# The selective-scan stage: TensorE's and ScalarE's loop over chunks written out in full, and the C rows loaded in quarters that GpSimd waits for one by one

## What is computed

```python
A = -jnp.exp(A_log)                     # (512 channels, 64 states)
C_used = C_ssm[:, jnp.arange(L) % 128, :]

def step(h, inp):
    dt, b, xt, c = inp
    dA = jnp.exp(dt[:, :, None] * A)
    h = dA * h + dt[:, :, None] * b[:, None, :] * xt[:, :, None]
    y = jnp.einsum('bdn,bn->bd', h, c)
    return (h, y)
...
return (y + x * D_param) @ out_proj_w.T
```

## Time and profile before

| | |
|---|---|
| time, median of 3 runs | 8651.39 us (8645.66 to 8653.18) |
| time of the profiled execution | 8648.8 us, its span 8647.0 us |
| TensorE busy | 7638.4 us (88%) |
| VectorE busy | 6621.9 us (77%) |
| GpSimd busy | 5670.5 us (66%) |
| ScalarE busy | 4702.7 us (54%) |
| scan stage, from its first scan to its last `reduce` | about 594.8 to 5550 us |

### The profile page before, as it was taken

How to read it: one execution, slowest core, us unless ns; L and a number is a source line. 1 busy time by engine, 2 the same in 40 slices (tenths; PEclk the granted TensorE clock), 3 DMA queues, 4 the chain that set the end, 5 groups by cost and what they waited for, 6 DMA issues and landing times. The chain is left out here.

```text
span 8647.0 us, 222908 instructions
## 1 busy us (share of the span) xinstructions
PE 7638.4 (88%) x76550; PEld 5615.1 (65%) x76550; DVE 6621.9 (77%) x8318; ACT 4702.7 (54%) x10584; POOL 5670.5 (66%) x3272
## 2 busy tenths in 40 slices
PE   5659999999989989989999999899999989999984
PEld 3337777777777777777777777644444436666653
DVE  4439999999999999999999999622222237878776
ACT  4447777777777777777777787511111112222220
POOL 0009999999999999999999999600000015554544
PEclk8779999999999999999999999999999988988885
DMA  3350000000000000000000000121221222222215
GB/s 134 137 158 0 20 21 0 20 21 1 19 21 20 0 21 20 0 21 20 8 13 20 20 0 5 60 83 68 87 82 68 92 79 78 76 79 74 79 66 168
DMA packets 198786, 423.53 MB, mean 49 GB/s; under 512 B 22448, under 2 KB 48496, under 8 KB 183024
## 3 DMA queue, kind: packets, MB, share of 16 engines
q1 hardware_dynamic: 172768, 382.77, 13.2%
q10 hardware_dynamic: 25872, 38.80, 1.2%
HBM read 225.11 MB, written 196.41 MB: 49 GB/s over the span
## 5 line engine op out<-in xcount | busy, mean ns | idle before, releaser
L485 POOL TENSOR_TENSOR scan_hc<-scan_h,scan_cb 128x1024 f32<-128x1024 f32 x2048 | 4776.9, 2366 | 265.8 <-DMA scan_cb<-scratch_bc 127.5
L651 DVE TENSOR_TENSOR_SCAN scan_h<-scan_a,scan_carry,scan_u 128x512 f32<-128x512 f32 x4096 | 4802.1, 1260 | 156.0 <-PE scan_u L590 128.1
L590 PE MATMUL scan_u<-scan_dg,scan_v 64*128 64x128 f32 x32768 | 2391.7, 286 | 339.1 <-DVE scan_h L651 280.1
L536 ACT ACTIVATE scan_a<-scan_dt,scan_aneg 128x512 f32<-128x512 f32 x4096 | 2659.9, 708 | 44.8 <-issue 30.5
L590 PEld LDWEIGHTS scan_u<-scan_dg,scan_v 64*128 64x128 f32 x32768 | 2000.7, 188 | 819.1 <-DVE scan_h L651 538.0
L598 PE MATMUL scan_y<-scan_ident,scan_hc 128*128 128x128 f32 x16408 | 2251.0, 280 | 60.1 <-POOL scan_hc L485 33.6
L598 PEld LDWEIGHTS scan_y<-scan_ident,scan_hc 128*128 128x128 f32 x16408 | 1764.8, 141 | 310.3 <-POOL scan_hc L485 34.5
L507 ACT ACTIVATE scan_dg<-scan_half,scan_bt 128x64 f32<-128x64 f32 x4096 | 1139.2, 341 | 5.0 <-DVE scan_onward L634 5.0
L528 ACT ACTIVATE scan_carry<-scan_h,scan_onward 128x4 f32 (+1 forms) x1008 | 303.0, 301 | 1042.5 <-DVE scan_h L651 1042.5
L177 POOL TENSOR_TENSOR mid_r<-mid_ve,mid_half_neg 128x4 f32<-128x4 f32 x32 | 32.4, 1012 | 1271.4 <-DVE mid_ve L132 784.1
L1141 POOL TENSOR_TENSOR core_joint<-core_own 128x32 f32<-128x32 f32 x64 | 17.4, 272 | 621.2 <-DVE core_own L1271 536.6
(11 more groups left out here) (211 smaller groups left out, 7647.3 us busy)
## 6 DMA issues: line engine op xcount, KB each, us to landing
scratch_y<-scan_yo ACTq DMA_DIRECT2D x17, 1024.0 KB, 4.7
pre_x<-in_x SPq DMA_DIRECT2D x16, 1024.0 KB, 6.8
scratch_z<-pre_zt SPq DMA_DIRECT2D x16, 1024.0 KB, 3.9
scratch_dt<-pre_dt SPq DMA_DIRECT2D x16, 1024.0 KB, 4.6
scratch_vr<-pre_vr ACTq DMA_DIRECT2D x16, 1024.0 KB, 4.7
scan_dt<-scratch_dt SPq DMA_DIRECT2D x16, 1024.0 KB, 5.3
scan_v<-scratch_vr SPq DMA_DIRECT2D x32, 512.0 KB, 7.8
scan_z<-scratch_z SPq DMA_DIRECT2D x16, 1024.0 KB, 10.7
```

The source lines that it names most:

```text
L485: pool.tensor_tensor(hc[:, q].rearrange("p n (r j) -> p n r j", j=P), h[:, q].rearrange("p n (r j) -> p n r j", j=P), cb[:, bass.ds(b * NS ...
L536: ins = act.activation(a[:, q, n, :], dt[:, par, q, :], ACT.Exp, scale=aneg[:, q, bass.ds(m * 2 + n, 1)])
L590: mm = pe.matmul(u_ps[:, q % 2, g, k * HP:(k + 1) * HP, :], v[row, par, k, q, :], dg[row, buf, k], start=True, stop=True)
L651: ins = dve.tensor_tensor_scan(h[:, q, n, :], a[:, q, n, :], u_ps[:, q % 2, :, :, n].rearrange("p g t -> p (g t)"), carry[:, q, bass.ds(m ...
```

## The change

`by_chunk` no longer has a loop: all 16 chunks of TensorE's and ScalarE's program are written out, with a constant number in each. The inner loops over pairs stay. The load of C is cut: each 4 MB transfer becomes four of 1 MB (16 states each), with a semaphore for each of the first sequence's quarters and one for all of the second sequence's; the second sequence's are issued behind the inputs of chunk 1. GpSimd's first chunk becomes four loops of 8 pairs, each behind the wait for its quarter, and its wait for the second sequence's C stands in front of chunk 8.

```diff
@@ scan_phase
+    PARTS = 4
+    PART = NS // PARTS
-        y_out = sem("y_out"); cb_in = sem("cb_in"); z_used = sem("z_used")
+        y_out = sem("y_out"); cb_in = [sem(f"cb_in{i}") for i in range(PARTS)]; cb_rest = sem("cb_rest"); z_used = sem("z_used")
-        def by_chunk(eng, chunk):
-
-            if NCH > 2:
-                with eng.Fori(0, NCH // 2 - 1) as p:
-                    for par in range(2):
-                        chunk(p * 2 + par, par, p, False)
-            for par in range(2):
-                chunk(NCH - 2 + par, par, NCH // 2 - 1, par == 1)
+        def by_chunk(chunk):
+
+            for c in range(NCH):
+                chunk(c, c % 2, c // 2, c == NCH - 1)
             load(0, 0)
-            for b in range(B):
-                sp.dma_start(cb[:, b * NS:(b + 1) * NS, :], bc_s[b * KC, HP:HP + NS, 0:P].partition_broadcast(P)).then_inc(cb_in, 16)
+
+            def load_c(b, n):
+                sp.dma_start(cb[:, b * NS + n * PART:b * NS + (n + 1) * PART, :], bc_s[b * KC, HP + n * PART:HP + (n + 1) * PART, 0:P].partition_broadcast(P)).then_inc(cb_rest if b else cb_in[n], 16)
+            for n in range(PARTS):
+                load_c(0, n)
             load(1, 1)
+            for b in range(1, B):
+                for n in range(PARTS):
+                    load_c(b, n)
...
             pool.sem_inc(hc_ready, Q)
-            pool.wait_ge(cb_in, 16 * B)
             pool.wait_ge(filled, 5)
-            with pool.Fori(0, B) as b:
-                with pool.Fori(0, KC) as k:
-                    with pool.Fori(0, PAIRS) as m:
-                        for q in range(Q):
-                            i = (b * KC + k) * PER + m * Q + q
+
+            def items(c, b, first, pairs):
+                with pool.Fori(0, pairs) as k:
+                    m = first + k
+                    for q in range(Q):
+                        i = c * PER + m * Q + q
...
+            for n in range(PARTS):
+                pool.wait_ge(cb_in[n], 16)
+                items(0, 0, n * (PAIRS // PARTS), PAIRS // PARTS)
+            for b in range(B):
+                if b:
+                    pool.wait_ge(cb_rest, 16 * PARTS * (B - 1))
+                with pool.Fori(b == 0, KC) as k:
+                    items(b * KC + k, b, 0, PAIRS)
```

More of the change, by code:

```diff
@@ L472, in _ @@
             pool.sem_inc(hc_ready, Q)
-            pool.wait_ge(cb_in, 16 * B)
             pool.wait_ge(filled, 5)
-            with pool.Fori(0, B) as b:
-                with pool.Fori(0, KC) as k:
-                    with pool.Fori(0, PAIRS) as m:
-                        for q in range(Q):
-                            i = (b * KC + k) * PER + m * Q + q
[L481 to L489, removed]
+            def items(c, b, first, pairs):
[3 more added lines that the diff above has]
+                        i = c * PER + m * Q + q
+                        pool.wait_ge(h_ready, i + Q + 1)
+                        pool.wait_ge(hc_used, i + 1)
+                        hold(pool, ticks["pool"])
+                        pool.tensor_tensor(
+                            hc[:, q].rearrange("p n (r j) -> p n r j", j=P),
+                            h[:, q].rearrange("p n (r j) -> p n r j", j=P),
+                            cb[:, bass.ds(b * NS + m * 2, 2), :].rearrange("p n (x j) -> p n x j", x=1).broadcast_to([P, 2, T // P, P]), ALU.mult
+                        ).then_inc(hc_ready, 1)
+            for n in range(PARTS):
[6 more added lines that the diff above has]
+                    items(b * KC + k, b, 0, PAIRS)
         @block.scalar
@@ L562, in _ @@
             diagonals(0, 0, 0, [(k, n) for k in range(K) for n in range(2)]).then_inc(dg_ready, 1)
-            by_chunk(act, chunk)
+            by_chunk(chunk)
             copy_out(NCH)
@@ L621, in chunk @@
                         reduce((c + 1) * PER - Q + q, q)
-            by_chunk(pe, chunk)
+            by_chunk(chunk)
         @block.vector
```

## The result

The changed kernel takes 8542.07 us (median of 4 runs, 8539.83 to 8550.57), the kernel before 8650.39 us: ratio 0.9877, with a 95% interval of 0.986 to 0.9894, 108 us less. Run anew it took 8544.76 against 8651.33 us, ratio 0.9876 (0.9861 to 0.9891). The forecast was 8549, 101.8 us less.

A forecast was written before the change was run, and what follows sets the result against it. VectorE's path was taken to bound the scan stage. Outer loop 69.2 plus C in quarters 32.6 gave 101.8 us off the profiled 8648.8, 8547.0, plus 2.6 to the median: 8549 us, own range 8540 to 8560, wider range 8538 to 8583.

The forecast's parts named there:

- What bounds: Scan stage: VectorE's path sets the time, 1.172 us a scan and 303.06 us a plain chunk.
- The outer loop: TensorE and ScalarE in the scan: writing it out removes 6 branches at 11.5 us of code fetch, 69.2 us.
- chunks 14 and 15: Scan chunks already written out behind the loop; their 3.04 us stops were taken as the model for every new chunk change.
- C in quarters: Scan start: VectorE goes on at 607.35 us instead of 639.96, 32.6 us gained.
- 4 MB take 17.9 us and 1 MB 4.5 us: Load of C at the scan's start: estimate that puts the first quarter's landing at 599.9 us.
- before 602.6 us: Scan chunk 0: sign of a right forecast, GpSimd's first product starting by then.
- rival 1: Load of C: quarters land together at 613.3 us, gaining 18.9 instead of 32.6, 8563 us; 0.12 together with GpSimd loop costs.
- GpSimd's new loops: Scan stage: five new loop ends taken to cost nothing, upper bound 26 us.
- The sum: Whole kernel: 69.2 + 32.6 = 101.8 us less, giving 8549 us.
- The packets of instructions: Instruction fetch in the scan: packets should be fewer by the 3 that each branch fetched anew.
- Rival 3: Inner loops in new places no longer held, 11.5 us a branch back: 8883 us in core_phase, 8710 in scan; chance 0.05.
- the weighing of the notes: TensorE code fetch: the skill's 2048-instruction room would mean no loop gain; trace stalls were preferred, its two-page window doubted.

The follow-up runs named there:

- e1_unroll: The kernel before with only the outer chunk loop of TensorE and ScalarE written out, C still in two transfers with one wait; 8582.11 us, ratio 0.9932.
- e2_quarters: The changed kernel with the old chunk loop put back on TensorE and ScalarE, so only C in quarters is new; 8618.39 us, ratio 0.9963.
- e8_shift: The kernel before with TensorE clearing y_ps five times instead of once ahead of its outer loop, which moves the loop's code; 8605.5 us, ratio 0.9948.
- e7_body10: The changed kernel with TensorE's inner loop in rounds of 10 pairs, 960 passes (weight load plus matmul); 8613.26 us, ratio 0.9957.
- e9_copy_early: The changed kernel with ScalarE copying y_ps out before the fourth item's save and diagonals instead of behind them; 8544.38 us, ratio 0.9877.

## Why the prediction was right, step by step

**What bounds.** VectorE's path, as read. Its pace of 1.172 us a scan and the plain period of 303.05 us held in the changed kernel.

**The outer loop, 69.2 us.** Right in mechanism and size. The 15 chunks behind the first stop take 4615.06 us before (639.96 to 5255.02) and 4545.84 in the changed kernel (608.58 to 5154.42): 69.2 less, and `e1_unroll` has 68.8 beside its shorter stop for C. Taking the difference of the periods (11.5) and not the sum of the listed stops (10.9) was right: 11.5 measured. That chunks 14 and 15 are the measured model of all written-out chunks was right too. One step was silent on how the price divides: it is TensorE's to 7.8 us a branch and ScalarE's to 4.0 once TensorE is free.

**C in quarters, 32.6 us.** Right. VectorE goes on 12.6 us after its first scan in the changed kernel, where the forecast had 607.35 - 594.82 = 12.5, and before it was 639.96 - 594.82 = 45.1: 32.6 less. `e2_quarters` has the same 12.5 (594.46 to 606.99); its stage has only 30.7 us less, as its six branches cost 1.9 us more than before's (606.99 to 5223.98 us is 4616.99). The landing was sized less well. The step "4 MB take 17.9 us and 1 MB 4.5 us" puts the quarter 4.5 us behind `scan_z`. In the profile shown it is 7.5 (584.00 + 11.4 = 595.4 to 602.9), and 4.7 to 5.7 in the six other profiles with quarters. So GpSimd's first product, at 603.53, missed my sign "before 602.6 us". Part of that is the stage's later start: counted from VectorE's first scan it is 7.5 us, and the latest harmless start was 7.8. In this execution it was luck by 0.3 us; in the others GpSimd begins 4.0 to 6.7 us behind the first scan. The second quarter, issued about 0.5 us behind the first, lands 3.0 to 3.9 us after it in all seven profiles. So if the quarters share the engines in part, as rival 1 had it, they still don't land together.

**GpSimd's new loops, nothing.** Right: no stop at the quarters.

**The sum.** 101.8 forecast; 69.2 + 32.6 = 101.8 on VectorE's path, 102.7 in the stage from first to last instruction. The medians say 108 and, run anew, 107; single parts give 67 + 31 = 98. The phases behind the scan, whose work is the same, differ by up to 10 us between executions, and I don't claim the last 5 us either way.

**The packets of instructions.** Here the reading was wrong, at no cost. I had said that a branch fetches 3 packets anew, which would be 18 fewer; the page has 80 instead of 94, 14 fewer. The old loop fetches 9 in each round (54 from 1225 to 4880 us), that is its whole body. The written-out code has to be fetched too, once, so that only the difference goes.

**Rival 3, and the weighing of the notes.** Here the prediction was wrong without paying for it. It took length for what decides ("672 is well under 832") and set 11.5 us on each branch. `e8_shift` shows that 832 passes are held too, where they lie well, and `e7_body10` that a missed branch can cost 2.1. I had also written that the trace speaks against room for 2048 instructions on TensorE. The Trainium skill (Runtime: NRT & Kernel Launch, instruction fetch mechanics) gives that figure and pieces of 16 KB. The runs are in keeping with both: 61 packets are 1.00 MB, 16 KB each, and a body of 1664 weight loads and matmuls and a few per cent of other instructions is held or lost by a shift of 64, one of 1920 lost. The Trainium skill's same section also has a window of two pages of 256 instructions. That doesn't hold for TensorE here, as a body of 1152 is held in 16 places. What the forecast needed, that the old loop in its old place is lost each round, came from the rows and stood.

**Open.** Why a branch back stops TensorE for 5.0 us and then 4.2 in the outer loop and only for about 2.2 in `e7_body10`. The traces take it one step further. In both cases TensorE goes on 2.6 to 3.2 us after the packet with its next code begins to move: 1233.21 to 1236.23 us before, 706.72 to 709.60 in `e7_body10`. But before, that packet begins 2.0 us after TensorE has stopped, and in `e7_body10` 0.7 us ahead of the stop. It is so at all 6 branches (1.35 to 2.09 us after) and at all 32 (0.2 to 0.8 ahead). Why the fetch starts later in the outer loop, no run tells. At the second stop, too, a packet moves (1240.49 us). That the branch's target lies close to the end of a piece there is my guess; no run shows it. Why a move by 64 instructions decides isn't shown either: I tried one distance only, and I don't know where the pieces begin. Whether ScalarE's outer loop could be held in another place wasn't tried.

## What to carry to other kernels

When TensorE and ScalarE stop for 4 to 5 us with no releaser and packets of instructions move, as here, look for a branch to code that the engine no longer has. Count those branches, price one as the difference of two periods, and compare it with a place where the code runs straight on. Before a loop is written out, try to move it: for TensorE's loop of 832 passes 64 free instructions ahead of it did the same. And if two engines stall together, take both away before judging either.

A load that a long stage waits for at its start needs only its first part early. Cut it, issue the first part first, and price it against the consumer's next natural stop: beyond that more speed brings nothing, as a quarter that came 2.6 us earlier showed here.

## What the runs showed that I had not expected

- TensorE's loop of 832 passes a round was held after a move by 64 instructions: 7 packets of its code instead of 61 from 1225 to 5440 us, and 46 us less.
- ScalarE's stall of 5 us at each round cost 0 beside TensorE's and 4.0 us without it.
- With code that streams in all the time (30 packets in one chunk instead of 4) the stage lost only 2.1 us at each of TensorE's branches.
- The first quarter of C landed 7.5 us behind `scan_z` in one execution and 4.7 to 5.7 in six others, and VectorE went on 12.5 to 12.6 us behind its first scan in all of those with the copies in their old place.
- The phases with unchanged code take 1353 to 1363 us (`core_phase`) and 1502 to 1511 us (`mid_phase`) from one execution to the next. That hides the 5.5 us that the stage gains in `e9_copy_early`.
